# Letting the first expert tiles start from an early table, with both parts of W2 streamed

## The reference

```
xn = layernorm(x)
x  = x + gnn(xn, edges) + linear_attention(xn)
x  = x + moe(layernorm(x))          # top 2 of 8 experts for each row
# moe: y_e = gelu(LN(x) W1[e] + b1[e]) W2[e] + b2[e],  W1 256x1024, W2 1024x256
```

## Time and profile before

| what | value |
|---|---|
| median of three runs | 2016.74 us (2013.73 to 2023.2) |
| the profiled execution, its time | 2020.03 us |
| span of the profile | 2018.4 us |
| PE busy | 1602.1 us (79%) |
| DVE, ACT, POOL busy | 1096.2, 899.2, 1142.1 us |
| data moved by DMA | 318.32 MB |
| mean granted clock of PE | 0.885 |

### The profile page before, as it was taken

How to read it: one execution, slowest core, us unless ns; L and a number is a source line. 1 busy time by engine, 2 the same in 40 slices (tenths; PEclk the granted TensorE clock), 3 DMA queues, 4 the chain that set the end, 5 groups by cost and what they waited for, 6 DMA issues and landing times. The chain is left out here.

```text
span 2018.4 us, 34593 instructions
## 1 busy us (share of the span) xinstructions
PE 1602.1 (79%) x9473; PEld 1356.1 (67%) x9474; DVE 1096.2 (54%) x3020; ACT 899.2 (45%) x1840; POOL 1142.1 (57%) x1150
## 2 busy tenths in 40 slices
PE   6766676676867688887777456489999999999997
PEld 5544454454655455555555345379999999999996
DVE  6522222222445466666665688356666666666663
ACT  6611111111223333344453477156666666666663
POOL 3277777777777677777777257713333333333333
PEclk9888888888988899988888755689999999999998
DMA  8344444344357566677676578736555565556554
GB/s 222 111 133 121 115 117 120 116 117 121 105 174 228 190 201 210 200 223 217 203 216 195 152 253 270 222 96 130 135 129 127 135 133 130 133 127 133 134 129 86
DMA packets 189254, 318.32 MB, mean 158 GB/s; under 512 B 33468, under 2 KB 134316, under 8 KB 188104
## 3 DMA queue, kind: packets, MB, share of 16 engines
q0 software_dynamic: 78432, 202.04, 38.8%
q1 hardware_dynamic: 101904, 112.55, 18.1%
q10 hardware_dynamic: 8824, 2.61, 0.6%
HBM read 237.61 MB, written 80.26 MB: 157 GB/s over the span
## 5 line engine op out<-in xcount | busy, mean ns | idle before, releaser
L686 POOL DMA_INDIRECT w2s_lent<-z_d,edge_tabs_lent x784 | 775.3, 989 | 294.6 <-issue 248.0
L1761 PE MATMUL bank<-w2s_lent,G 128*128 x976 | 280.3, 439 | 111.5 <-POOLq L674 111.4
L1296 DVE TENSOR_TENSOR acc_lent<-acc_lent,bank 128x258 f32 x244 | 102.4, 420 | 471.6 <-PE bank L1761 465.9
L1761 PE MATMUL bank<-w2s_lent,S_lent 128*128 x976 | 272.0, 428 | 83.4 <-POOLq L674 80.3
L1761 PEld LDWEIGHTS bank<-w2s_lent,G 128*128 128x128 f32 x976 | 207.0, 218 | 176.7 <-issue 139.5
L1761 PEld LDWEIGHTS bank<-w2s_lent,S_lent 128*128 128x128 f32 x976 | 201.9, 212 | 148.7 <-issue 114.6
L728 POOL DMA_INDIRECT out_dram<-G,acc_lent x112 | 178.4, 1593 | 203.1 <-DVE G L1622 125.3
L1020 ACT ACTIVATE G<-bank,acc_lent 128x256 f32<-128x256 f32 x448 | 188.0, 471 | 195.8 <-PE bank L1948 109.6
L1601 DVE TENSOR_TENSOR acc<-w1s,acc 128x512 fp32r<-128x512 f32 x224 | 155.0, 693 | 204.6 <-ACT acc L1007 185.3
L1969 PE MATMUL bank<-w2s,acc 128*128 x896 | 262.9, 293 | 2.4 <-DMA edge_tabs<-w2lo_d 2.4
L1946 PE MATMUL bank<-acc 128*128 128x256 f32 x896 | 257.8, 288 | 3.7 <-DVE acc L1609 3.7
(11 more groups left out here) (314 smaller groups left out, 2856.2 us busy)
## 6 DMA issues: line engine op xcount, KB each, us to landing
S<-w2lo_d POOLq DMA_DIRECT2D x56, 512.0 KB, 4.0
edge_tabs<-w2lo_d POOLq DMA_DIRECT2D x56, 512.0 KB
acc_lent<-bucket_d SPq DMA_DIRECT2D x56, 266.0 KB, 3.0
w2s_lent<-z_d,edge_tabs_lent POOLq DMA_INDIRECT x784
bu_d<-w2s_lent SPq DMA_DIRECT2D x98, 128.0 KB, 1.9
w2s_lent<-bu_d SPq DMA_DIRECT2D x12, 768.0 KB, 8.7
w1s<-in_L_ffn_W_dram SPq DMA_DIRECT2D x8, 1024.0 KB, 6.9
w2s_lent<-in_L_ffn_W_dram SPq DMA_DIRECT2D x32, 256.0 KB, 5.4
```

What stands on the lines that cost most here:

```text
L686: pool.indirect_dma_start(out=ring_rows[:, row % (RING * QUAD), 0:D], out_offset=None, in_=z_d[:, :], in_offset=bass.IndirectOffsetOnAxis( ...
L1761: m = pe.matmul(bank[j % DEPTH][:, 0:ACCW], S_of[j % DEPTH][:, k, :], rows[:, ds(bases[j], ACCW)], start=(k == 0), stop=(k == QUAD - 1))
```

## The change

Part by part:

- After the counts of groups 0 to 2 are there, DVE makes a first table (`early_tiles`) that lists six tiles (EARLY = 6) out of the whole tiles of 256 rows that these groups have already filled. This is done at the end of DVE's turn 4. The table is turned by PE ahead of its turn 6 and stored by DVE at the end of turn 6, with `sel` (`early_set`).
- PE begins the experts after its last `r_logits`: it transposes tile 0, does `r_rank` of group 8, 24 WARM multiplications in place of 56, and goes on with tiles. ACT and DVE split the first W1 before the last group's exponentials and placement.
- The table of the rest is made in the middle of the first tiles (`last_tiles`, `last_set`); nothing after tile 5 starts without it. All eight padding blocks are written by SP, between the loads of rows for tiles 2 and 3. Tiles from 6 on wait for all scatters.
- W2's high part is no longer kept on chip. `w2_d` in DRAM holds both parts side by side, and `load_w2l` loads halves of 1024 KB (high and low part of half the expert). The first two are issued by POOL between the scatters of groups 7 and 8.
- The hidden values, the transposed rows and the W2 buffers move to the room that W2 had; `W1_FREE` becomes group 4 instead of 5. The u and b parts of groups 2 to 8 are loaded into other places.

The same rows are computed in the same number of tiles (56).

```
+EARLY = 6
+EARLY_GROUP = 2
+WARM = 24
-        w2hi_d = dram("w2hi_d", (EXPERTS, P, HC * D))
-        w2lo_d = dram("w2lo_d", (EXPERTS, P, HC * D))
+        w2_d = dram("w2_d", (EXPERTS, P, 2 * HC * D))
...
-        w2l = [S_r[:, :, :, :].rearrange("p a b n -> p (a b n)"), edge_tabs_r[:, 0:HC * D // 2]]
+        w2l = [inw2s(HC * D) for _ in range(2)]
...
@@ SP
+            sp.wait_ge(s["moetab_set"], 1)
+            for g in (EARLY_GROUP - 1, EARLY_GROUP):
+                sp.wait_ge(pair["scattered"][g % 2], scattered_by(g))
+            for t in range(3):
+                load_xe(t, t % 2, t // 2)
             sp.wait_ge(s["padpos_ready"], 1)
-            for e in range(0, EXPERTS, 2):
+            for e in range(EXPERTS):
                 pad_rows(sp, e)
+            for t in range(3, EARLY):
+                load_xe(t, t % 2, t // 2)
             sp.wait_ge(s["zrows"], 16 * 3)
             sp.wait_ge(s["pads_out"], 16 * EXPERTS)
             for h in range(2):
                 sp.wait_ge(pair["scattered"][h], SCATTERED[h])
+            sp.wait_ge(s["moetab_set"], 2)
+            repeat(sp, None, load_xes, EARLY // 2, MOE_TILES // 2)
@@ POOL
-            w2_after = {1: (2, 3), 2: (7,), 4: (6,), 5: (4, 5), 7: (0, 1)}
             for g in range(GROUPS):
+                if g == GROUPS - 1:
+                    pool.wait_ge(s["moetab_set"], 1)
+                    for half in range(2):
+                        load_w2l(0, half)
                 scatters(g)
-                for e in w2_after.get(g, ()):
-                    load_w2(pool, e, e + 1, s["w2_in"])
-                n = HC * D // 2
+                n = HC * D
@@ DVE
             for g in range(1, GROUPS):
                 r_x1(g)
                 if g + 1 < GROUPS:
                     r_y(g + 1)
                 r_pick(g - 1)
                 r_scale(g)
                 r_place(g - 1)
+                if g == EARLY_GROUP + 2:
+                    early_tiles()
+                if g == EARLY_GROUP + 4:
+                    early_set()
             r_pick(GROUPS - 1)
+            dve.wait_ge(s["moetab_set"], 1)
...
             e0 = expert_of(dve, 0)
             for q in range(MOE_PARTS):
                 first_weights(0, q, e0)
+            r_place(GROUPS - 1)
             turned(0, 0, e0)
+            moe(-1, 1)
+            last_tiles()
+            moe(0, 0)
+            moe(1, 1)
+            last_set()
@@ PE
+            pe.wait_ge(s["moetab_set"], 1)
+            pe.wait_ge(s["sel_ready"], 1)
             turn_x(0, 0, 0)
+            r_rank(GROUPS - 1)
+            for _ in range(WARM):
+                pe.matmul(bank[7][:, :], before[:, :], ones_b[:, :]...)
             moe(-1, 1)
+            counts_mm(GROUPS, bank[5][:, 64:64 + EXPERTS])
+            moe(0, 0)
+            table_mm(2, bank[5][:, P:3 * P])
+            moe(1, 1)
+            for turn in range(1, EARLY // 2 - 1):
+                two(turn)
+            pe.wait_ge(s["moetab_set"], 2)
+            repeat(pe, None, two, EARLY // 2 - 1, MOE_TILES // 2 - 1)
```

More of the change, by code:

```diff
@@ L59 @@
 MOE_PARTS = 4
-WARM = 56
+EARLY = 6
+EARLY_GROUP = 2
+WARM = 24
 OUT_ROWS = NT * P + P
@@ L1586, in _, with whole_tiles @@
-            L.after(dve.memset(sel[:, :, :], 0.0))
-            for e in range(EXPERTS):
-                a = dve.tensor_scalar(sel[0:96, e, :], pm[0:96].to_broadcast([96, P]), float(e), None, ALU.is_equal)
-            a.then_inc(s["sel_ready"], 1)
-            dve.wait_ge(s["moetab_set"], 1)
-            dve.wait_ge(s["fold_done"], 2 * EXPERTS)
-            for g in (W1_FREE - 1, W1_FREE):
-                dve.wait_ge(pair["scattered"][g % 2], scattered_by(g))
+            def whole_tiles(counts, rounded):
+                L.after(dve.tensor_scalar(ci, counts, float(rounded), None, ALU.add))
+                L.after(dve.tensor_scalar(ci, ci, 8, None, ALU.logical_shift_right))
+                L.after(dve.tensor_copy(ntf, ci))
@@ new lines, in early_set @@
+            def early_set():
+                dve.wait_ge(s["mtab_mm"], 1)
+                dve.wait_ge(pair["scattered"][0], scattered_by(0))
+                dve.tensor_copy(moetab[0:1, :], bank[4][0:1, D:D + 2 * P]).then_inc(s["moetab_set"], 1)
+                L.after(dve.memset(sel[:, :, :], 0.0))
+                for e in range(EXPERTS):
+                    a = dve.tensor_scalar(sel[0:96, e, :], pm[0:96].to_broadcast([96, P]), float(e), None, ALU.is_equal)
+                a.then_inc(s["sel_ready"], 1)
@@ L1644, in moe @@
                         turned(i + 2, par, e)
+            r_x1(0)
+            r_scale(0)
+            for g in range(1, GROUPS):
+                r_x1(g)
+                if g + 1 < GROUPS:
+                    r_y(g + 1)
+                r_pick(g - 1)
+                r_scale(g)
+                r_place(g - 1)
+                if g == EARLY_GROUP + 2:
+                    early_tiles()
+                if g == EARLY_GROUP + 4:
+                    early_set()
+            r_pick(GROUPS - 1)
+            dve.wait_ge(s["moetab_set"], 1)
+            dve.wait_ge(s["fold_done"], 2 * EXPERTS)
+            for g in (W1_FREE - 1, W1_FREE):
+                dve.wait_ge(pair["scattered"][g % 2], scattered_by(g))
             e0 = expert_of(dve, 0)
@@ L1903, in r_rank, with counts_mm, table_mm @@
                 follow()
+            def counts_mm(groups, to):
+                pe.wait_ge(s["pay_ready"], groups)
+                pe.matmul(to, ones_b[:, :], cnt[:, :], start=True, stop=True).then_inc(s["mtab_cnt"], 1)
+            def table_mm(n, to):
+                pe.wait_ge(s["mtab_ready"], n)
+                for k in range(2):
+                    m = pe.matmul(to[0:1, k * P:(k + 1) * P], tile_table[:, k:k + 1], ident[:, :], start=True, stop=True)
+                m.then_inc(s["mtab_mm"], 1)
             for g in range(GROUPS):
+                if g == EARLY_GROUP + 2:
+                    counts_mm(EARLY_GROUP + 1, bank[4][:, 0:EXPERTS])
+                if g == EARLY_GROUP + 4:
+                    table_mm(1, bank[4][:, D:D + 2 * P])
                 if g:
@@ L1994, in two @@
                 moe(2 * turn + 1, 1)
+            pe.wait_ge(s["moetab_set"], 1)
+            pe.wait_ge(s["sel_ready"], 1)
             turn_x(0, 0, 0)
+            r_rank(GROUPS - 1)
+            for _ in range(WARM):
+                pe.matmul(bank[7][:, :], before[:, :], ones_b[:, :].rearrange("p (o n) -> p o n", o=1).to_broadcast([P, 4, P]),
+                          start=True, stop=True)
             moe(-1, 1)
-            repeat(pe, None, two, 0, MOE_TILES // 2 - 1)
+            counts_mm(GROUPS, bank[5][:, 64:64 + EXPERTS])
+            moe(0, 0)
+            table_mm(2, bank[5][:, P:3 * P])
+            moe(1, 1)
+            for turn in range(1, EARLY // 2 - 1):
+                two(turn)
+            pe.wait_ge(s["moetab_set"], 2)
+            repeat(pe, None, two, EARLY // 2 - 1, MOE_TILES // 2 - 1)
             moe(MOE_TILES - 2, 0)
```

174 lines of the change are left out of this document (81 added, 93 removed).

## The result

The changed kernel takes 1998.82 us (median of six runs, 1996.61 to 2005.0) against 2015.97 us for the kernel before (six runs, 2013.73 to 2023.2): ratio 0.9913, 95% interval 0.9897 to 0.9929, so faster by 17.2 us. The forecast was 1994 us, faster. The profiled execution took 1996.61 us (span 1994.9 us), 23.5 us less span than the one before, but the medians differ by 17.

| stretch | before | after | change | forecast |
|---|---|---|---|---|
| start to DVE's first x1 operation of group 0 | 1141.45 | 1133.94 | -7.5 | 0 |
| from there to the first layer1 product | 179.06 | 147.92 | -31.1 | -29.0 |
| to DVE's cast of tile 5's rows | 55.8 | 61.5 | +5.7 | +4.6 |
| fifty tiles, to the cast of tile 55 | 602.83 | 608.76 | +5.9 | +1 |
| to the last product | 26.26 | 27.06 | +0.8 | 0 |

What follows compares the result with a forecast made beforehand. PE was taken to bound the experts, DVE the routing, and POOL's queue the end of the gap between. Terms -29.0 - 2.2 + 0.8 + 6 + 1 = -23.4 us from 2016.7 gave 1993.3, stated as 1994 us; range 1980 to 2035.

Steps and rivals of the forecast that it cites:

- Head start: Between routing and experts: layer1 of tile 0 starts at 1291.5 instead of 1320.51 us, -29.0 us.
- the term -2.2: First 24 layer1 products: full clock with WARM right before them, 5.0 - 2.9 = -2.2 us; bound 0.
- DVE's 5.4 us: DVE's routing turns 4 and 6: early table 3.2 and `early_set` 2.2 us delay all later routing; bounds 0 and 7.
- First tiles' waits: First tiles: waits for W2 halves and rows beside scatters and padding, +6 us, bounds 0 and 14.
- the slow spell of the clock behind each wait: First tiles: PE's slower clock after a wait, counted inside the +6 us.
- The wait for the rows of tile 3: First tiles: rows issued after the padding land at 1318 to 1324, wanted at 1320: wait 0 to 4 us.
- W2 in every tile: All tiles: 1024 KB halves land in 5.4 to 6.1 us, within about 6.6 us of room; +1 us.
- The dearest rival: All tiles: W2 lands late in each; a landing of 8.2 us costs 88 us, 2080; chance 0.17 for slower.
- a tile at 12.05 us: Steady experts: what the profile after would show for each tile, 12.05 us.
- stray ones: Steady tiles: occasional late W2 landings, +1 us.
- likeliest case: Whole kernel: the forecast itself, 1986 to 2001 us, chance 0.52.

Runs made afterwards that it cites:

- r_after2: The changed kernel, unedited, run and profiled again on a chip of the first kind: 2000.62 us, ratio 0.9925 to the kernel before.
- e_hold: The changed kernel, but SP loads expert rows only after all scatters landed and PE transposes tile 0 after WARM: 2240.17 us, ratio 1.0098, second kind of chip.
- e_double: The changed kernel with two pairs of W2 buffers, tiles 0 and 1's halves issued ahead of group 8's scatters: 1993.49 us, ratio 0.9891, first kind of chip.
- r_before: The kernel before, unedited, profiled again on a chip of the second kind: 2224.46 us, one run.
- e_double_h: The changed kernel with two pairs of W2 buffers and the hidden values back in `acc`: 2185.98 us, ratio 0.9897 to the kernel before, second kind of chip.
- e_double_h_sel: The changed kernel with two W2 buffer pairs, hidden values in `acc`, and `sel` made after tile 0's cast: 2185.34 us, ratio 0.9895, second kind of chip.
- r_after: The changed kernel, unedited, profiled again on a chip of the second kind: 2218.99 us, one run.

## Why the prediction was right, and where it was off

**Head start, -29.0 forecast, -31.1 measured.** The steps held: rows of the first groups were there in time, the first layer1 product came 11.1 us after the last router product ended (forecast 11.2), and the products began at full clock (the first 24 start over 2.95 us, not 5.04; the term -2.2). WARM took 6.94 us (forecast 6.4). The 2.1 us beyond the forecast are luck: in this profile, alone of the five of changed kernels on the first kind of chip, the router products of group 7 took 2.86 us at a granted clock of 0.98, where `r_after2` and the kernel before have 5.23 at 0.50. `r_after2` has -28.7. `e_hold` shows that this is the part that makes the kernel faster: without it the ratio is 1.0098, on the second kind of chip.

**DVE's 5.4 us.** The two pieces took 2.8 and 2.1 us (forecast 3.2 and 2.2). DVE's turn 8 begins 5.5 to 6.1 us later than before in all five profiles of changed kernels on the first kind of chip (117.4 to 117.9 us behind group 0's x1, against 111.8), so the term was right. The last router product starts 5.7 to 6.3 us later in four of them (138.8 to 139.4 against 133.1), and 3.4 in the pair above, by the fast products of group 7. On the other kind it is 163.2 to 166.2 against 161.5. So DVE's row does set the routing's pace on the first kind.

**First tiles' waits, +6 forecast.** With the clock and the small products the stretch was +5.7 for +4.6. It is one wait: 4.19 us for tile 1's half of W2 (forecast 1.5, at most 6), and the slow products behind it, in the prediction's own words the slow spell of the clock behind each wait. The wait for the rows of tile 3 (forecast 0 to 4) did not come on the first kind of chip. Counted from group 0's x1, POOL issued the half at 166.9 us (forecast 163.6) and PE wanted it at 173.6 (forecast 170.2), as much later. So what the forecast had too small is the landing, 10.7 us beside the padding and the last scatters where it had 8. `e_double`, with the halves issued ahead of those, takes 5.5 us off.

**W2 in every tile, landing 5.4 to 6.1 forecast.** It lands in 5.4 us, inside the 6.6 us that the tile gives, and no tile is late as a rule. The dearest rival is dead. DMA share 0.78 and 214 GB/s (forecast 0.83 and 220). The Trainium skill, DMA: Bandwidth & Descriptors, section "Bandwidth", has 6.15 us of engine time for 1 MB from GpSimd. The trace disagrees: the whole landing took 5.4 us, and 5.1 at best.

**The step that failed: "a tile at 12.05 us".** I costed the move of the hidden values at nothing. The tile became 0.08 us longer, 3.9 us over fifty. Neither half the bytes nor no loads at all brought it back; the hidden values in `acc` brought 0.06 of the 0.08 back, in three kernels on two chips. The last 0.02 have no run. This, not the streaming, is most of what the steady part lost. The other 2.0 us are the two tiles with a late W2, where I had +1 for stray ones.

**Not forecast either:** +0.8 us to the last product, and +2.7 us behind it, where POOL adds the last rows. The tail varied between 15.0 and 19.8 us in the other changed kernels and was 14.8 in `r_before`, so I give it no cause.

The sum by measured terms: -31.1 + 5.7 + 5.9 + 0.8 + 2.7 = -16.0 us, where I had -23.4. By `r_after2`: -28.7 + 5.3 + 3.9 + 3.7 for the last two = -15.8. So the forecast held in its direction and its main term, and the time lies in its likeliest case (1986 to 2001); what it left out is the tile's term and a longer tail.

**How far it holds.** On chips of the second kind the same change gave 4.7 us in one pair of profiles. There the tiles lost about the same; the difference is the early part: 18.5 us instead of 11.5 from the last router product to layer1, the wait for the late rank, and an early stretch of 68.5. Half the bytes brought that stretch to 60.4 and W2 loaded once to 58.5. But `e_hold`, with all of W2, has 60.4 too, and `e_double_h`, which moves as many bytes in the steady part and more ahead of it, 58.3. So it isn't the bytes as such but what they meet, and which transfer holds up the rows of tile 3 was not separated. These are single profiles.

**The best version.** `e_double` beats the changed kernel by 7.1 us on the first kind (ratio to before 0.9891), `e_double_h_sel` and `e_double_h` have 0.9895 and 0.9897 on the second. They were not run on the first kind; with the fifty tiles' 3.0 us taken from `e_double`'s 1993.49 they would be near 1990 us there, an estimate.

## What to carry to other kernels

A transfer that ran in the shadow of PE cost nothing here as long as its landing fitted the time between last use and next use: a tile took 12.14 us with it and without it, at a DMA share of 0.78. Work out that time from two rows; it decides more than the share. Where work starts earlier, it meets the traffic that it used to wait for: issue the first loads ahead of the burst and give them a buffer of their own (5.5 us here). When an edit moves an operand to another place, put a term for it in the sum, as small as it looks, times the number of tiles.

## What was not expected of the hardware

- The layer2 products of PE started 1 to 2 ns further apart with the hidden values in the array that W2 is read from than in the other one (119.9 against 118.2 ns in the mean, 12.14 against 12.08 us a tile). With the transposed rows put back in `acc` the step behind the first product of layer1 fell from 121.7 to 118.9 ns, other steps grew, and the tile did not get shorter. Whether it is the array, the address or something else was not separated.
- Two kinds of chips: the part ahead of group 0 took 1134 to 1142 us or 1298 to 1317 us for the same instructions, and a tile of the changed kernel 12.14 us on both. On the second kind the semaphore of PE's rank came up to 9.0 us behind the product that sets it, on the first 0.01.
- In three profiles (the first of after, `r_after`, `e_hold`) the only slow tile of the steady part was number 31 (in the first also 32), 12.43 to 13.23 us; in the others none was. The cause is open.
